# Expert routing over quads of tiles: a deeper software pipeline, and its row-wise passes on ScalarE

## The chip, the cores and the metric

The kernel runs on one core of one Trainium2 chip. The metric is the device time of the whole program in microseconds (us). Engine names in the profile: PE is TensorE, DVE is VectorE, ACT is ScalarE, POOL is GpSimd, SP is SyncE (here it only issues DMAs). Each engine runs its own instructions in the order in which they are written; between engines there are only semaphores.

## The reference

The model is a token encoder, an attention layer and a mixture-of-experts layer over 16 x 256 = 4096 tokens of width 128. The change touches only the routing of the last layer: a layer norm, 64 logits per token, a softmax, the 42 largest probabilities of 64, and a second softmax over those 42.

```python
h = h + _L0_ffn_ref(_layernorm(h, axis=-1), w1, b1, w2, b2, router_w, router_b)

def _L0_ffn_ref(x, w1, b1, w2, b2, router_w, router_b):     # E, H, K = (64, 256, 42)
    logits = x @ router_w + router_b
    probs = jax.nn.softmax(logits, axis=-1)
    top_w, top_idx = jax.lax.top_k(probs, K)
    top_w = jax.nn.softmax(top_w, axis=-1)
    ...
    comb = jnp.zeros((N, E), x.dtype).at[jnp.arange(N)[:, None], top_idx].set(top_w)
    h = jax.nn.gelu(jnp.einsum('td,edh->teh', xt, w1) + b1, approximate=False)
    y = jnp.einsum('teh,ehd->ted', h, w2) + b2
    out = jnp.einsum('ted,te->td', y, comb)
```

## The kernel before

The program is a row of blocks, one after the other: embedding, projections, attention, `route`, `experts`. Between two blocks all engines meet at a barrier. `h` holds the residual stream, 32 tiles of 128 tokens x 128, and `mv` each token's mean and variance.

`route` goes over 8 quads of 4 tiles (`QT = 4`, `GT = 512` tokens). For a quad q:

- DVE `norm` (L1501): four passes of 128x128 give the normed tiles `r_xn`.
- PE `turn_x` (L1571): four transposes into PSUM `r_ps_x`.
- ACT `copy_x` (L1459, L1460): PSUM to `x_s` and again to `x_hi` (the high part for the experts). POOL (L1482) makes `x_lo`.
- PE `logit` (L1579, L1580): for each tile one matmul with the router's weights and one with its bias (a contraction of one row). In the trace each of the 8 matmuls is two instructions.
- DVE `probabilities`: the negative row maximum (L1510), `d1` = logits less the maximum (L1512); ACT takes the exponent of it for the whole quad, 128x256 (L1470); DVE sums (L1515), takes the reciprocal (L1516), the negated probabilities `neg_p` (L1517) and `d2` (L1518); ACT takes the second exponent (L1473).
- DVE `choose`: with `neg_p` it finds the 22 experts to drop, 8 at a time, by MAX8 and MATCH_REPLACE8 (L1536, L1538). It then masks the second exponent (`top`, L1543), sums it (L1545), takes the reciprocal `r2` (L1546) and multiplies (`comb`, L1548).
- PE `turn_comb` (L1588): four transposes; ACT `copy_comb` (L1465) copies to `comb_t`, and SP writes it to the DRAM array `comb_rows` (L1438).

What runs beside what is set by the order in which each engine's steps are written. DVE's pass over quad q is max, `d1`, `norm(q + 1)`, sum to `d2`, `choose(q)`; PE's is `turn_x(q)`, `logit(q)`, `turn_comb(q - 1)`; ACT's is `copy_x(q)`, first exponent of q, `copy_comb(q - 1)`, second exponent of q. Two quads are written out, then a register loop runs over pairs of quads (`repeat`); on DVE the last two are written out again. `hold` is a wait followed by a no-op when the awaited value is in a register.

SP has in its queue, ahead of the rows: the loads of the router's weights and of the first experts' weights. After the rows of quads 0 to 3 it loads four 1 MB tiles `c_row` (L1642), broadcast from `comb_rows`, then writes the rows of quads 4 to 7. POOL splits two experts' weights (`split_weights`) after its last `x_lo`.

`experts` then makes three-part matmuls of 512 columns over 64 experts in two sweeps, and nothing of it is touched.

Of the kernel before, what the change touches and what calls it, by code (L numbers as in the profile page):

```python
# [7 lines left out]
F32 = mybir.dt.float32  # L8
# [3 lines left out]
ALU = mybir.AluOpType  # L12
# [1350 lines left out]
def route(nc, h, ident, ones_row, router_rev, router_b_rev, mv, rstd, x_hi, x_lo, comb_t, comb_rows, f, loader):  # L1363

    QT = GT // P
    QUADS = TILES // QT
    with ExitStack() as ctx:
# [9 lines left out]
        root = sb("r_root", [P, TILES])  # L1383
        xn = sb("r_xn", [P, 2, QT, DIM])
        x_s = sb("x_s", [P, 2, GT])
        neg_max = sb("r_neg_max", [P, QT])
        d1 = sb("d1", [P, QT, EXPERTS])
        e1 = sb("e1", [P, QT, EXPERTS])
        neg_s1 = sb("neg_s1", [P, QT])
        neg_r1 = sb("neg_r1", [P, QT])  # L1390
        neg_p = sb("neg_p", [P, QT, EXPERTS])
        d2 = sb("d2", [P, QT, EXPERTS])
        e2 = sb("e2", [P, QT, EXPERTS])
        left = sb("left", [P, QT, EXPERTS])
        low = sb("low", [P, QT, 8])
        top = sb("top", [P, QT, EXPERTS])
        s2 = sb("s2", [P, QT])
        r2 = sb("r2", [P, QT])
# [7 lines left out]
        rstd_ready = sem("r_rstd_ready")  # L1406
# [7 lines left out]
        d1_ready = sem("d1_ready")  # L1414
        exp_one = sem("exp_one")
        d2_ready = sem("d2_ready")
        exp_two = sem("exp_two")
        sum_step = sem("sum_step")
        top_step = sem("top_step")
        comb_ready = sem("comb_ready")  # L1420
# [4 lines left out]
        def cols(q):  # L1425
            return bass.ds(q * GT, GT)

        def spread(of_tile):
            return of_tile[:].unsqueeze(2).broadcast_to([P, QT, EXPERTS])
# [21 lines left out]
        @block.scalar  # L1451
        def _(act):
            act.wait_ge(var_eps, 1)
            act.activation(root[:], shifted[:], ACT.Sqrt).then_inc(rooted, 1)

            def copy_x(q, b):
                act.wait_ge(turned, q + 1)
                after(act, x_used, q - 1)
                act.activation(x_s[:, b], ps_x[:, b], ACT.Copy).then_inc(x_copied, 1)  # L1459
                act.activation(x_hi[:, cols(q)], ps_x[:, b], ACT.Copy).then_inc(hi_ready, 1)  # L1460

            def copy_comb(q, b):
                if in_range(q, QUADS):
                    hold(act, comb_turned, q + 1)
                    act.activation(comb_t[:, cols(q)], ps_c[0:EXPERTS, b], ACT.Copy).then_inc(comb_copied, 1)  # L1465
# [10 lines left out]
            copy_comb(QUADS - 1, 1)  # L1476

        @block.gpsimd
        def _(pool):
            def step(q, b):  # L1480
                pool.wait_ge(hi_ready, q + 1)
                pool.tensor_tensor(x_lo[:, cols(q)], x_s[:, b], x_hi[:, cols(q)].bitcast(F32), ALU.subtract  # L1482
                                   ).then_inc(x_used, 1)

            repeat(pool, step, QUADS)
            for r in range(SPLIT_EARLY):
                split_weights(pool, f, r, r, 32)

        @block.vector
        def _(dve):  # L1490
            dve.tensor_scalar(shifted[:], mv[:, :, 1], LN_EPS, None, ALU.add).then_inc(var_eps, 1)
            dve.wait_ge(rooted, 1)
            dve.reciprocal(rstd[:], root[:]).then_inc(rstd_ready, 1)
            dve.wait_ge(rstd_ready, 1)

            def norm(q, b):
                if in_range(q, QUADS):
                    after(dve, turned, q - 1)
                    for k in range(QT):
                        t = q * QT + k  # L1500
                        last = dve.tensor_scalar(xn[:, b, k, :], h[:, t, :], mv[:, t, 0:1], rstd[:, bass.ds(t, 1)],  # L1501
                                                 ALU.subtract, ALU.mult)
                    last.then_inc(normed, 1)

            def probabilities(q, b):

                of_quad = ps_l[:, b, 0:QT * EXPERTS].rearrange("p (k e) -> p k e", k=QT)
                link = chained(dve, sum_step, q * 3)
                dve.wait_ge(logits, q + 1)
                dve.tensor_reduce(neg_max[:], of_quad, AX.X, ALU.max, negate=True).then_inc(max_ready, 1)  # L1510
                hold(dve, max_ready, q + 1)
                dve.tensor_tensor(d1[:], of_quad, spread(neg_max), ALU.add).then_inc(d1_ready, 1)  # L1512
                norm(q + 1, 1 - b)
                dve.wait_ge(exp_one, q + 1)
                link(dve.tensor_reduce(neg_s1[:], e1[:], AX.X, ALU.add, negate=True))  # L1515
                link(dve.reciprocal(neg_r1[:], neg_s1[:]))  # L1516
                link(dve.tensor_tensor(neg_p[:], e1[:], spread(neg_r1), ALU.mult))  # L1517
                dve.tensor_tensor(d2[:], neg_p[:], spread(neg_r1), ALU.subtract).then_inc(d2_ready, 1)  # L1518

            def choose(q, b):  # L1520

                halves = (range(0, QT // 2), range(QT // 2, QT))
                before = q * STEPS
                rounds = [(taken, op) for taken in range(0, DROPPED, 8) for op in ("max", "marks", "take")
                          if op != "marks" or DROPPED - taken < 8]
                for n, (taken, op) in enumerate(rounds):
                    source = left if taken else neg_p
                    for half, tiles in enumerate(halves):
                        if n:
                            hold(dve, top_step, before + (2 * (n - 1) + half + 1))  # L1530
# [8 lines left out]
                        last.then_inc(top_step, 1)  # L1539
                link = chained(dve, top_step, before + 2 * len(rounds))  # L1540
                hold(dve, top_step, before + 2 * len(rounds))
                dve.wait_ge(exp_two, q + 1)
                link(dve.scalar_tensor_tensor(out=top[:], in0=left[:], scalar=MARK, in1=e2[:], op0=ALU.is_gt,  # L1543
                                              op1=ALU.mult))
                link(dve.tensor_reduce(s2[:], top[:], AX.X, ALU.add))  # L1545
                link(dve.reciprocal(r2[:], s2[:]))  # L1546
                after(dve, comb_turned, q - 1)
                dve.tensor_tensor(comb[:, b], top[:], spread(r2), ALU.mult).then_inc(comb_ready, 1)  # L1548

            def step(q, b):  # L1550
                if not isinstance(q, int) or q > 0:
                    hold(dve, comb_ready, q)
                probabilities(q, b)
                choose(q, b)

            ROUNDS = -(-DROPPED // 8)
            STEPS = 2 * (2 * ROUNDS + 1) + 3
            norm(0, 0)
            repeat(dve, step, QUADS - 2)
            for q in (QUADS - 2, QUADS - 1):  # L1560
                step(q, q % 2)

        @block.tensor
        def _(pe):
            pe.wait_ge(loads, 32)

            def turn_x(q, b):
                pe.wait_ge(normed, q + 1)
                after(pe, hi_ready, q - 1)
                for k in range(QT):  # L1570
                    last = pe.transpose(ps_x[:, b, k * P:(k + 1) * P], xn[:, b, k, :], ident[:])  # L1571
                last.then_inc(turned, 1)
# [347 lines left out]
```

## Time and profile before

| | us |
|---|---|
| runs, median of 3 | 2085.62 (2084.45 to 2085.73) |
| the profiled execution, its own time | 2084.88 |
| its span in the trace | 2083.0 |
| blocks before `route` | 0 to 571.2 |
| `route` | 571.2 to 662.5 |
| `experts` | 662.5 to 2083.0 |

Reading it: the profiled execution took 1.88 us more than the span of its trace, and its time lies 0.74 us under the median. The trace's rows show for each instruction its start and its duration; a row with x4 merges four instructions, and its duration is from the first start to the last end. In brackets stands the engine's idle time before the row and what ended it. The granted TensorE clock is given as a share of 2.4 GHz, so 0.50 is 1.2 GHz.

### The profile page before, as it was taken

What the parts mean: (1) busy time and instruction counts of PE and PEld (TensorE: products, weight loads), DVE (VectorE), ACT (ScalarE), POOL (GpSimd) and SP (SyncE); (2) the same over time, 40 slices, a digit from 0 to 9 for tenths busy, and PEclk for the clock granted to TensorE, in tenths of its full rate; (3) what the DMA queues carried; (4) which work ended last, traced back from release to release, by engine and by line L of the source; (5) the groups of instructions that cost most, each with busy time, mean ns of one, the idle gap of its engine ahead of it and who ended that gap; (6) DMA issues with size and microseconds to landing.
All of it is one profiled execution on the core that took longest, in us unless ns stands there. A gap on an engine that the chain in (4) does not pass through costs nothing.

```text
span 2083.0 us, 29167 instructions
## 1 busy us (share of the span) xinstructions
PE 1844.9 (89%) x8486; PEld 1461.0 (70%) x8486; DVE 1828.0 (88%) x2358; ACT 1454.8 (70%) x2558; POOL 682.5 (33%) x439
## 2 busy tenths in 40 slices
PE   5455658878766999999999999999999999999998
PEld 3333335555554888888888888878888888888887
DVE  8435558888677999999999999979999999999997
ACT  2145546666522888888888888878888888888886
POOL 4250015445312233333333333323333333333330
PEclk9967769899955999999999999999999999999999
DMA  7410000000012333333333333323333333333331
GB/s 207 136 41 0 1 1 1 0 0 0 1 34 96 126 121 108 124 126 126 113 113 126 126 124 109 119 101 126 117 112 124 126 126 111 116 126 126 123 108 56
DMA packets 105256, 191.46 MB, mean 92 GB/s; under 512 B 13558, under 2 KB 86246, under 8 KB 88550
## 3 DMA queue, kind: packets, MB, share of 16 engines
q1 hardware_dynamic: 103166, 186.77, 26.1%
q0 software_dynamic: 2048, 4.20, 0.7%
q8 instruction: 18, 0.29, 0.1%
q14 instruction: 24, 0.20, 0.0%
HBM read 179.40 MB, written 11.53 MB: 92 GB/s over the span
## 4 chain that ended last, share of the span: by engine, by line
PE 67%; DVE 0%; issue 0%; ACT 0%; DVEq 0%; ACTq 0%
PE f_ps_h L1837 11%; PE f_ps_h L1838 11%; PE f_ps_h L1839 11%; PE f_ps_y L1848 11%; PE f_ps_y L1849 11%; PE f_ps_y L1850 11%; PE f_ps_y L1863 0%; DVE s_lo L1793 0%; DVE scaled L1787 0%; PE f_ps_h L1874 0%; ACT act_out L1748 0%; DVE h L1811 0%; ACT y_t L1772 0%; DVEq L1669 0%; PE f_ps_h L1819 0%
## 5 line engine op out<-in xcount | busy, mean ns | idle before, releaser
L1748 ACT ACTIVATE act_out<-f_ps_h,b_t 128x512 f32<-128x512 f32 x1024 | 649.6, 686 | 257.4 <-PE f_ps_h L1839 257.4
L1787 DVE TENSOR_TENSOR scaled<-act_out,c_row 128x1024 f32<-128x1024 f32 x512 | 753.0, 1471 | 42.7 <-ACT act_out L1748 42.2
L1793 DVE TENSOR_TENSOR s_lo<-scaled,s_hi 128x1024 fp32r<-128x1024 f32 x512 | 672.7, 1314 | 0.1
L1756 ACT ACTIVATE s_hi<-scaled 128x1024 fp32r<-128x1024 f32 x512 | 541.9, 1058 | 2.3 <-DVE scaled L1787 1.5
L1651 POOL CAST w_hi<-w_raw 128x512 fp32r<-128x512 f32 x128 | 200.7, 1568 | 909.8 <-PE f_ps_y L1850 898.0
L1837 PE MATMUL f_ps_h<-x_hi,w_hi 128*128 x1024 | 399.8, 390 | 2.2 <-DVE h L1811 1.5
L1848 PE MATMUL f_ps_y<-s_hi,w_hi 128*128 128x512 f32 x1024 | 398.7, 389 | 3.0 <-DVE s_lo L1793 3.0
L1838 PE MATMUL f_ps_h<-x_lo,w_hi 128*128 x1024 | 399.4, 390 | 0.0
L1839 PE MATMUL f_ps_h<-x_hi,w_lo 128*128 x1024 | 399.2, 390 | 0.0
L1850 PE MATMUL f_ps_y<-s_hi,w_lo 128*128 128x512 f32 x1024 | 398.4, 389 | 0.0
L1849 PE MATMUL f_ps_y<-s_lo,w_hi 128*128 128x512 f32 x1024 | 398.4, 389 | 0.0
L1653 POOL TENSOR_TENSOR w_lo<-w_raw,w_hi 128x512 fp32r<-128x512 f32 x128 | 271.0, 2117 | 10.2
L1837 PEld LDWEIGHTS f_ps_h<-x_hi,w_hi 128*128 128x128 f32 x1024 | 192.7, 188 | 44.1 <-issue 4.1
L1848 PEld LDWEIGHTS f_ps_y<-s_hi,w_hi 128*128 128x128 f32 x1024 | 192.2, 188 | 44.5 <-DVE s_lo L1793 4.6
L1839 PEld LDWEIGHTS f_ps_h<-x_hi,w_lo 128*128 128x128 f32 x1024 | 192.8, 188 | 40.2
L1838 PEld LDWEIGHTS f_ps_h<-x_lo,w_hi 128*128 128x128 f32 x1024 | 192.8, 188 | 39.9
L1850 PEld LDWEIGHTS f_ps_y<-s_hi,w_lo 128*128 128x128 f32 x1024 | 192.2, 188 | 40.0
L1849 PEld LDWEIGHTS f_ps_y<-s_lo,w_hi 128*128 128x128 f32 x1024 | 192.2, 188 | 39.6
L1203 POOL TENSOR_TENSOR sm<-sm,rinv 128x1024 f32<-128x1024 f32 (+1 forms) x32 | 88.1, 2752 | 122.3 <-DVE rinv L1258 122.3
L1168 ACT ACTIVATE sm<-sm,neg_max 128x128 f32<-128x128 f32 (+1 forms) x256 | 112.7, 444 | 16.4 <-DVE neg_max L1252 16.3
L1189 POOL TENSOR_TENSOR qkn<-qk,rms 128x640 f32 (+1 forms) x32 | 40.3, 1260 | 158.4 <-SPq L1089 149.1
L1160 ACT ACTIVATE p_t<-ps_p 128x1024 f32<-128x1024 f32 x48 | 49.1, 1023 | 59.4 <-PE ps_p L1296 59.4
(219 smaller groups left out, 1652.7 us busy)
## 6 DMA issues: line engine op xcount, KB each, us to landing
c_row<-comb_rows SPq DMA_DIRECT2D x128, 1024.0 KB, 4.8
w_raw<-in_w SPq DMA_DIRECT2D x256, 128.0 KB, 4.3
by_slot<-b_zeros SPq DMA_DIRECT2D x1, 3072.0 KB, 13.4
b_gauss_s<-by_slot SPq DMA_DIRECT2D x12, 256.0 KB, 5.3
mixed_rows<-b_mixed SPq DMA_DIRECT2D x12, 256.0 KB, 2.3
out<-h SPq DMA_DIRECT2D x8, 256.0 KB, 4.7
cent<-in_centers SPq DMA_DIRECT2D x1, 1536.0 KB, 7.1
neg_prec<-in_logvar SPq DMA_DIRECT2D x1, 1536.0 KB, 10.9
```

The source lines that it names most:

```text
L1651: pool.tensor_copy(w_hi[:, r], w_raw[:, r]).then_inc(f["hi_copied"], 1)
L1653: pool.tensor_tensor(w_lo[:, r], w_raw[:, r], w_hi[:, r].bitcast(F32), ALU.subtract).then_inc(f["w_split"], 1)
L1748: last = act.activation(act_out[:, r % 2, c, :], ps_h[:, r % 2, c, :], ACT.Gelu, bias=b1_t[:, c, bass.ds(e, 1)])
L1756: act.activation(s_hi[:, r % RING], scaled[:, r % RING], ACT.Copy).then_inc(hi_ready, 1)
L1787: dve.tensor_tensor(scaled[:, r % RING], act_out[:, r % 2], c_row[:, k, g * GT:(g + 1) * GT].unsqueeze(1).broadcast_to([P, HC, GT]), ALU.m ...
L1793: dve.tensor_tensor(s_lo[:, r % RING], scaled[:, r % RING], s_hi[:, r % RING].bitcast(F32), ALU.subtract).then_inc(lo_ready, 1)
L1837: pe.matmul(to, w_hi[:, k, 0, at], x_hi[:, tokens(w, g)], start=True, stop=False)
L1838: pe.matmul(to, w_hi[:, k, 0, at], x_lo[:, tokens(w, g)], start=False, stop=False)
L1839: last = pe.matmul(to, w_lo[:, k, 0, at], x_hi[:, tokens(w, g)], start=False, stop=True)
L1848: pe.matmul(ps_y[:, g, :], w_hi[:, k, 1, at], s_hi[:, slot, c, :], start=False, stop=False)
L1849: pe.matmul(ps_y[:, g, :], w_hi[:, k, 1, at], s_lo[:, slot, c, :], start=False, stop=False)
L1850: last = pe.matmul(ps_y[:, g, :], w_lo[:, k, 1, at], s_hi[:, slot, c, :], start=False, stop=last_step and c == HC - 1)
```

## The change

Nothing is computed differently up to rounding. The register loops go: all 8 quads are written out on every engine. These steps move from DVE to ACT, and the 128x256 exponents are cut into one instruction for each tile, since ACT's scale and bias operands hold one number per row:

- `norm`: ACT.Identity with scale `rstd` and a new bias `r_shift` = -mean x rstd (one DVE pass of 128x32 at the start).
- `first_exps`: the exponent reads PSUM with the negative maximum as bias, and sums its row by `accum_out`; `d1` and DVE's sum (L1515) go. One small DVE pass of 128x4 turns s1 into -s1.
- `second_exps`: bias `neg_r1` takes the place of `d2`.
- `weigh`: ACT multiplies `top` by `r2` and gives `comb`.

A one-element exponent (`warm`) after the square root has the exponent's table loaded at once. The buffers between these steps are doubled. In line numbers of the changed kernel:

```diff
-            def step(q, b):
-                copy_x(q, b)
-                act.wait_ge(d1_ready, q + 1)
-                act.activation(e1[:], d1[:], ACT.Exp).then_inc(exp_one, 1)
-                copy_comb(q - 1, 1 - b)
-                act.wait_ge(d2_ready, q + 1)
-                act.activation(e2[:], d2[:], ACT.Exp, scale=-1.0).then_inc(exp_two, 1)
-            repeat(act, step, QUADS)
+            act.activation(warm[:], shifted[:, 0:1], ACT.Exp, scale=0.0)
+            def norm(q):
...
+                    act.wait_ge(ln_ready, 1)
+                    after(act, turned, q - 1)
+                    for k in range(QT):
+                        t = q * QT + k
+                        last = act.activation(xn[:, q % 2, k, :], h[:, t, :], ACT.Identity, scale=rstd[:, t:t + 1],
+                                              bias=shift[:, t:t + 1])
+                    last.then_inc(normed, 1)
+            def first_exps(q):
...
+                    act.wait_ge(max_ready, q + 1)
+                    for k in range(QT):
+                        last = act.activation(e1[:, b, k, :], ps_l[:, b, k * EXPERTS:(k + 1) * EXPERTS], ACT.Exp,
+                                              bias=neg_max[:, b, k:k + 1], accum_out=s1[:, b, k:k + 1])
+                    last.then_inc(exp_one, 1)
+            def second_exps(q):
...
+                    act.wait_ge(p_ready, q + 1)
+                    for k in range(QT):
+                        last = act.activation(e2[:, b, k, :], neg_p[:, b, k, :], ACT.Exp, scale=-1.0,
+                                              bias=neg_r1[:, b, k:k + 1])
+                    last.then_inc(exp_two, 1)
+            def weigh(q):
...
+                    act.wait_ge(r2_ready, q + 1)
+                    after(act, comb_turned, q - 1)
+                    for k in range(QT):
+                        last = act.activation(comb[:, b, k, :], top[:, b, k, :], ACT.Copy, scale=r2[:, b, k:k + 1])
+                    last.then_inc(comb_ready, 1)
+            norm(0)
+            copy_x(0)
+            norm(1)
+            first_exps(0)
+            copy_x(1)
+            second_exps(0)
+            norm(2)
+            for s in range(QUADS + 2):
+                first_exps(s + 1)
+                copy_x(s + 2)
+                weigh(s - 1)
+                norm(s + 3)
+                copy_comb(s - 2)
+                second_exps(s + 1)
...
+            maximum(0)
+            probabilities(0)
+            for q in range(QUADS):
+                maximum(q + 1)
+                after(dve, comb_ready, q - 1)
+                choose(q)
+                probabilities(q + 1)
...
+            turn_x(0)
+            logit(0)
+            turn_x(1)
+            logit(1)
+            for s in range(QUADS + 1):
+                turn_x(s + 2)
+                logit(s + 2)
+                turn_comb(s - 1)
```

How the instructions stand on ACT before, one quad inside the register loop (the names in brackets are the semaphores waited for):

```order
L1459 ACTIVATE x_s<-r_ps_x 128x512 [waits x_used,r_turned]
L1460 ISA
L1460 ACTIVATE x_hi<-r_ps_x 128x512
L1470 ACTIVATE e<-d 128x256 [waits d1_ready]
L1465 REGISTER_ALU [waits comb_turned]
L1465 ACTIVATE comb_t<-r_ps_c 64x512 [waits comb_turned]
L1473 ACTIVATE e<-d 128x256 [waits d2_ready]
```

And on ACT after the change, one pass in the middle (s = 2, so the rows are of quads 3, 4, 1, 5, 0 and 3):

```order
L1476 ACTIVATE e,s<-ps_l,r_neg_max 128x64 [waits r_max_ready]
L1476 ACTIVATE e,s<-ps_l,r_neg_max 128x64 x3
L1468 ACTIVATE x_s<-r_ps_x 128x512 [waits x_used,r_turned]
L1469 ACTIVATE x_hi<-r_ps_x 128x512
L1495 ACTIVATE comb<-top,r 128x64 [waits r2_ready]
L1495 ACTIVATE comb<-top,r 128x64 x3
L1459 ACTIVATE r_xn<-h,r_shift,rstd 128x128 [waits r_turned,r_ln_ready]
L1459 ACTIVATE r_xn<-h,r_shift,rstd 128x128 x3
L1501 ACTIVATE comb_t<-r_ps_c 64x512 [waits comb_turned]
L1485 ACTIVATE e<-neg_p,neg_r 128x64 [waits p_ready]
L1485 ACTIVATE e<-neg_p,neg_r 128x64 x3
```

ACT goes from 5 to 19 activations for a quad, and `x_s` of quad q + 2 now stands behind the first exponents of quad q + 1.

On DVE before, from the end of `choose(0)` to the start of `choose(1)`:

```order
L1543 SCALAR_TENSOR_TENSOR top<-left,e 128x256 [waits exp_two,top_step]
L1545 TENSOR_REDUCE s<-top 128x4 [waits top_step]
L1546 RECIPROCAL r<-s 128x4 [waits top_step]
L1548 TENSOR_TENSOR comb<-top,r 128x256 [waits top_step]
L1510 TENSOR_REDUCE r_neg_max<-ps_l 128x4 [waits logits,comb_ready]
L1512 TENSOR_TENSOR d<-ps_l,r_neg_max 128x256 [waits r_max_ready]
L1501 TENSOR_SCALAR r_xn<-h,mv,rstd 128x128 [waits r_turned]
L1501 TENSOR_SCALAR r_xn<-h,mv,rstd 128x128 x3
L1515 TENSOR_REDUCE neg_s<-e 128x4 [waits exp_one]
L1516 RECIPROCAL neg_r<-neg_s 128x4 [waits sum_step]
L1517 TENSOR_TENSOR neg_p<-e,neg_r 128x256 [waits sum_step]
L1518 TENSOR_TENSOR d<-neg_p,neg_r 128x256 [waits sum_step]
```

On DVE after the change, from the end of `choose(1)` to the start of `choose(2)`, the last row being the first MAX8:

```order
L1579 SCALAR_TENSOR_TENSOR top<-left,e 128x256 [waits exp_two,top_step]
L1581 TENSOR_REDUCE s<-top 128x4 [waits top_step]
L1582 RECIPROCAL r<-s 128x4 [waits top_step]
L1549 SCALAR_TENSOR_TENSOR neg_s<-s 128x4 [waits exp_one]
L1551 RECIPROCAL neg_r<-neg_s 128x4 [waits p_step]
L1552 TENSOR_TENSOR neg_p<-e,neg_r 128x256 [waits p_step]
L1540 TENSOR_REDUCE r_neg_max<-ps_l 128x4 [waits logits]
L1573 MAX low<-neg_p 128x8 [waits p_ready,comb_ready]
```

Eight passes have left DVE between two searches (four of them `norm`), one small one has come, and the maximum of quad q + 1, with its wait for the logits, now stands ahead of `choose(q)`.

## Rows read from the trace of the kernel before

**Rows 1.** Busy time, granted clock and DMA of two stretches: `route`, and `experts`.
```profile
core 0: us, PE busy (x) PEld busy (x) DVE busy (x) ACT busy (x) POOL busy (x), PEclk, DMA share, GB/s
571.20:662.50 91.30, 57.10 (x192) 41.93 (x192) 71.77 (x418) 21.68 (x43) 13.99 (x12) 0.51 0.20 70
662.50:2083.00 1420.50, 1408.97 (x6194) 1160.53 (x6194) 1366.64 (x1033) 1140.88 (x1546) 467.67 (x252) 1.00 0.33 116
```
**Rows 2.** The list of waits in `route`: total us, times, longest.
```profile
DVE r_neg_max L1510 <- PE ps_l L1580: 7.9, 3, 7.0
```
**Rows 3.** Timeline, start of `route`: start us, duration us, engine, instruction.
```profile
571.28 1.28 ACT L1454 ACT_TABLE_LOAD   x1 [5.67 <-PEq L1089]
...
572.58 0.23 ACT L1454 ACTIVATE r_root<-r_shifted 128x32 f32<-128x32 f32 x1
...
576.26 0.69 PE L1579 MATMUL ps_l<-rw,x_s 128*128 128x64 f32 x2 [0.69 <-ACT x_s L1459]
...
576.71 1.28 ACT L1470 ACT_TABLE_LOAD   x1
...
581.30 0.42 DVE L1510 TENSOR_REDUCE r_neg_max<-ps_l 128x4 f32<-128x256 f32 x1 [6.96 <-PE ps_l L1580]
```
**Rows 4.** Timeline of the last quad and the end of `route`.
```profile
651.08 0.43 DVE L1510 TENSOR_REDUCE r_neg_max<-ps_l 128x4 f32<-128x256 f32 x1
...
653.92 0.60 DVE L1536 MAX8 low<-neg_p 128x8 f32<-128x64 f32 x4
...
658.04 0.43 DVE L1543 SCALAR_TENSOR_TENSOR top<-left,e 128x256 f32<-128x256 f32 x1
...
659.17 0.43 DVE L1548 TENSOR_TENSOR comb<-top,r 128x256 f32<-128x256 f32 x1
...
659.74 1.03 PE L1588 MATMUL r_ps_c<-ident,comb 128*64 128x128 f32 x4 [7.51 <-DVE comb L1548]
660.81 0.59 ACT L1465 ACTIVATE comb_t<-r_ps_c 64x512 f32<-64x512 f32 x1 [6.36 <-PE r_ps_c L1588]
```
**Rows 5.** Timeline of PE inside the register loop, one quad.
```profile
625.28 0.69 PE L1579 MATMUL ps_l<-rw,x_s 128*128 128x64 f32 x2 [1.49 <-ACT x_s L1459]
...
629.60 0.69 PE L1580 MATMUL ps_l<-rb,ones_row 1*128 1x64 f32 x2
630.61 1.03 PE L1588 MATMUL r_ps_c<-ident,comb 128*64 128x128 f32 x4 [0.33 <-DVE comb L1548]
632.67 1.11 PE L1571 MATMUL r_ps_x<-ident,r_xn 128*128 128x128 f32 x4 [1.03 <-DVE r_xn L1501]
```
**Rows 6.** Groups of instructions in `route`: busy us, mean ns, idle before.
```profile
L1516 DVE RECIPROCAL neg_r<-neg_s 128x4 f32<-128x4 f32 x8 | 1.4, 178 | 0.6
L1517 DVE TENSOR_TENSOR neg_p<-e,neg_r 128x256 f32<-128x256 f32 x8 | 3.4, 425 | 0.6
L1459 ACT ACTIVATE x_s<-r_ps_x 128x512 f32<-128x512 f32 x8 | 4.7, 586 | 2.8 <-PE r_ps_x L1571 2.8
```
**Rows 7.** Timeline of ACT in attention: exponents with bias and row sum, 128x128.
```profile
509.29 0.39 ACT L1168 ACTIVATE sm<-sm,neg_max 128x128 f32<-128x128 f32 x1
509.59 0.19 ACT L1168 ACTIVATION_READ_ACCUMULATOR sm<-sm,neg_max 128x1 f32 x1
509.68 0.39 ACT L1168 ACTIVATE sm<-sm,neg_max 128x128 f32<-128x128 f32 x1
```
**Rows 8.** Timeline of ACT in the projections: a scaled copy of 64 columns.
```profile
151.22 0.31 ACT L881 ACTIVATE qk<-p_ps_rkv,p_kv_rms 128x64 f32<-128x64 f32 x1
151.42 0.23 ACT L882 ACTIVATE qk<-p_ps_rkv 128x64 f32<-128x64 f32 x1
```
**Rows 9.** Group, whole trace: ACT's layer norm of the projections.
```profile
L842 ACT ACTIVATE p_xn<-h,p_shift,p_rstd 128x128 f32<-128x128 f32 x32 | 13.7, 565 | 0.4 <-DVE p_shift L927 0.4
```
**Rows 10.** Timeline of DVE while POOL splits weights.
```profile
649.65 1.40 DVE L1548 TENSOR_TENSOR comb<-top,r 128x256 f32<-128x256 f32 x1
```
**Rows 11.** SP's issue of the four `c_row` loads, and the stretch in which they land.
```profile
624.99 2.00 SPq L1642 DMA_DIRECT2D c_row<-comb_rows  x4
...
625.00:637.00 12.00, 8.79 (x30) 6.64 (x30) 10.71 (x71) 3.09 (x7) 2.28 (x2) 0.50 0.91 360
```

More of the change, by code:

```diff
@@ L1505, in probabilities @@
[L1505 to L1518, printed above, removed]
@@ L1538, in choose @@
                                 last = dve.match_replace(left[:, k, :], low[:, k, :], source[:, k, :], MARK)
-                        last.then_inc(top_step, 1)
-                link = chained(dve, top_step, before + 2 * len(rounds))
-                hold(dve, top_step, before + 2 * len(rounds))
+                        mark(last)
+                settle()
                 dve.wait_ge(exp_two, q + 1)
-                link(dve.scalar_tensor_tensor(out=top[:], in0=left[:], scalar=MARK, in1=e2[:], op0=ALU.is_gt,
+                link(dve.scalar_tensor_tensor(out=top[:, b], in0=left[:], scalar=MARK, in1=e2[:, b], op0=ALU.is_gt,
                                               op1=ALU.mult))
[L1545 to L1561, printed above, removed]
+                link(dve.tensor_reduce(s2[:], top[:, b], AX.X, ALU.add))
+                dve.reciprocal(r2[:, b], s2[:]).then_inc(r2_ready, 1)
+            maximum(0)
+            probabilities(0)
+            for q in range(QUADS):
+                maximum(q + 1)
+                after(dve, comb_ready, q - 1)
+                choose(q)
+                probabilities(q + 1)
         @block.tensor
@@ L1565, in _ @@
             pe.wait_ge(loads, 32)
[L1567 to L1572, printed above, removed]
-            def logit(q, b):
-                pe.wait_ge(x_copied, q + 1)
-                after(pe, d1_ready, q - 1)
-                for k in range(QT):
-                    of_tile = ps_l[:, b, k * EXPERTS:(k + 1) * EXPERTS]
-                    pe.matmul(of_tile, x_s[:, b, k * P:(k + 1) * P], rw[:], start=True, stop=False)
-                    last = pe.matmul(of_tile, ones_row[:], rb[:], start=False, stop=True)
-                last.then_inc(logits, 1)
@@ L1583, in turn_comb, with turn_x, logit @@
-            def turn_comb(q, b):
+            def turn_x(q):
+                if in_range(q, QUADS):
+                    pe.wait_ge(normed, q + 1)
+                    after(pe, hi_ready, q - 1)
+                    for k in range(QT):
+                        last = pe.transpose(ps_x[:, q % 2, k * P:(k + 1) * P], xn[:, q % 2, k, :], ident[:])
+                    last.then_inc(turned, 1)
+            def logit(q):
+                if in_range(q, QUADS):
+                    b = q % 2
+                    pe.wait_ge(x_copied, q + 1)
+                    after(pe, exp_one, q - 1)
+                    for k in range(QT):
+                        of_tile = ps_l[:, b, k * EXPERTS:(k + 1) * EXPERTS]
+                        pe.matmul(of_tile, x_s[:, b, k * P:(k + 1) * P], rw[:], start=True, stop=False)
+                        last = pe.matmul(of_tile, ones_row[:], rb[:], start=False, stop=True)
+                    last.then_inc(logits, 1)
```

111 lines of the change are left out of this document (63 added, 48 removed).

## The prediction

> **What bounds the kernel now.** I read the windows by stage first [rows 1]. `route` takes 91.3 us of 2083, PE's clock is granted at 0.51 there (1.2 GHz), and DVE is the busiest engine with 71.8 us; in `experts` PE is busy for 1409 of 1420.5 us at 1.00. Nothing in `experts` is edited, so the change is worth what it takes off `route`. The list of waits says who drives it [rows 2]: DVE waited 7.9 us in all for logits, 7.0 of them before the first quad. From then on DVE hardly stops, so DVE's own pass is the pace. The timeline gives that pace: the first of eight row maxima starts at 581.30 [rows 3], the last at 651.08 [rows 4]: 69.78 us for 7 quads, 9.97 each. So `route` before is a start (571.28 to 581.30), 69.78 us of pace, and a tail from the last maximum to the end of the last ACT copy (651.08 to 661.40, 10.32 us) [rows 4]. I cost each of the three.
>
> **The pace after the change.** Four loops could set it. I take each from rows and keep the longest; M(q) is the start of quad q's maximum.
>
> *DVE's pass.* Maximum 0.43 + 0.04 of gap. From the first MAX8 to the masked exponent 4.12 (653.92 to 658.04), from there to the end of `r2` 1.10 (to just before 659.17) [rows 4]. Then the small pass of 128x4, which no row here shows and which I take as the reciprocal of the same shape, 0.18, the reciprocal 0.18, and `neg_p` 0.43 [rows 6], with gaps 0.9. Sum 6.6 us.
>
> *PE's pass.* The eight steps of the logits are issued 0.617 apart (625.28 to 629.60 is seven of them), so 4.93; four `comb` transposes last 1.03 alone and four `x` transposes 1.11 [rows 5]. In a queue the first four give way earlier: one transpose alone is some 0.42 of the 1.03, so four follow each other in 0.82. PE's queue is still `turn_x`, `logit`, `turn_comb`, and between `turn_x` and `logit` of one quad stands ACT's copy `x_s`, 0.59 [rows 6]. PE has no other quad's work to put there. Sum 4.93 + 0.82 + 1.11 + 0.59 + 0.1 for two hand-overs = 7.55 us.
>
> *The loop through ACT.* `x_s` of quad q + 2 is queued behind the first exponents of q + 1, and these behind M(q + 1). An exponent with row sum starts 0.39 after the one before at 128 columns (509.29 to 509.68) [rows 7]; I take 0.33 at 64, four in 1.33. Bounds for the four are 1.33 and 4 x (0.39 + 0.19) = 2.3 if nothing overlaps. Maximum 0.43 + 1.33 + `x_s` 0.59 + logits and hand-over 5.04 (576.26 to 581.30) [rows 3] + 0.1 = 7.5 us. It is level with PE's pass.
>
> *The loop over two quads.* ACT's second exponents of q + 1 wait for DVE's pass, and ahead of `x_s` of q + 3 stand they and the first exponents of q + 2. A scaled copy of 64 columns lets the next start after 0.20 and lasts 0.31 [rows 8], so four in 0.93. DVE's pass 6.6 + 0.93 + 1.42 + 0.59 + 5.04 = 14.6 for two quads, 7.3 each. It is closed, but 0.25 a quad short of deciding.
>
> ACT's own work, overlapped, is 1.33 + 1.1 (two copies) + 0.85 + 1.7 (`norm`: 13.7 us for 32 [rows 9]) + 0.55 + 0.85 = 6.4 us. It has a reserve of 1.1 us per quad.
>
> So PE and its round trip to ACT take over from DVE: 7 x 7.55 = 52.9 us in place of 69.8, **-16.9 us**. What DVE gave away above 0.9 us per quad is not earned. Removing the register loops is in these numbers, since I used the rows of the written-out last quad.
>
> **Two rules weighed.** Does PE stay at 1.2 GHz? PE runs 6.0 us of logits and transposes with one gap of 0.33 (625.28 to 631.64) [rows 5], eight times over, and the clock's mean over the block stays 0.51 [rows 1]. After the change the same instructions run with fewer gaps, so I keep 1.2 GHz. The Trainium skill (TensorE: Matmul & The Clock Gate, "What's actually happening") says that sustained matmul activity releases the throttle. By it the clock would rise, now that PE's gaps shrink, and the sum would be that of the first rival below. The Trainium skill (ScalarE: Activation LUTs, "Rules for kernel authors") advises VectorE, not ScalarE, for multiplications and additions. For the work itself the trace agrees: 256 columns are 0.43 us on DVE [rows 6] and 0.93 in four pieces on ACT [rows 8]. It costs here only where ACT is on the path, which is the tail.
>
> **The start, later.** The root ends at 572.81 [rows 3]. The exponent's table load of 1.28, hidden under the logits before (576.71) [rows 3], now stands ahead of `norm(0)`: 574.1, plus the one-element exponent, 0.2 by the root beside it. `norm(0)` on ACT takes 13.7 / 32 x 4 = 1.7: 576.0. Transposes 1.11, `x_s` 0.59, logits 5.04 and hand-overs: M(0) = 582.9. That is **+1.6 us**. DVE then waits before `choose(0)`, since the maximum of quad 1 stands ahead of it. M(1) is still one loop through ACT later (7.5), so this wait moves work into the tail and does not lengthen the pace.
>
> **The tail, longer.** `choose(6)`, which before lay ahead of the last maximum, now lies behind it. From M(7): maximum 0.47, `choose(6)` 5.27, probabilities 0.85, `choose(7)` 5.22, `weigh` on ACT 0.93 (0.43 on DVE before), transposes 1.03, copy 0.59, hand-overs 0.15: 14.5 us in place of 10.3, **+4.2 us**. Here the first exponents and `comb`'s copies have no cover at all; all else on ACT is covered by DVE's search.
>
> **Moved and hidden.** POOL's weight split slows DVE passes with two tensors: `comb` took 1.40 in place of 0.43 beside it [rows 10]. It now falls near the sixth quad, where DVE has 0.9 us of reserve; I take 0, with 0.7 late if it misses. SP's `c_row` loads wait for `comb` of quad 3. They were issued at 624.99 and took about 12 us [rows 11]. `comb_t` of quad 3 now leaves near 632 and is written by 635, so they land near 647, before `experts` starts near 650. What is queued behind them on SP is only the writing of rows of the second sweep. The waits `exp_one` and `comb_ready` on PE and DVE are met 3 us early in this schedule. If the burst slows something, it costs at most what it lasts beyond 650: nothing to 3 us.
>
> **Sum.** +1.6 - 16.9 + 4.2 = -11.1 us. Against the profiled execution's own 2084.88 that is 2073.8; against the median of the runs, 0.74 higher, 2074.5. I say **2074.2**. With a pace of 7.45 to 7.95 (hand-overs smaller, or 0.4 more each quad) this case runs from 2073 to 2077.5.
>
> **Rivals.**
>
> 1. *PE's clock rises.* Then PE's pass shrinks (logits between half of 5.04 and 5.04) and DVE's 6.6 is the pace from M(1): 7.5 + 6 x 6.6 = 47.1, -22.7. Sum -16.9: **2068**. For it: PE's gaps shrink to one of 0.65 us in a pass. Against: eight stretches of 6 us without a rise. Chance 0.14.
> 2. *The passes run longer than their parts*, 8.5 in place of 7.55: hand-overs on a three-engine loop, ACT starting its pieces later than the 0.33, written-out code that must be fetched while `c_row` fills the DMA engines (share 0.91 [rows 11]). 59.5 of pace, -10.3; sum -4.5: **2080**. For it: with three loops within 0.25 us of each other, a delay in any is felt. Against: written-out quads showed no gaps. Chance 0.14.
> 3. *Slower: ACT becomes the bound.* If its short instructions do not overlap, ACT pays whole durations for a quad: first exponents 2.3, two copies 1.2, `weigh` 1.24, `norm` 4 x 0.565 = 2.26 [rows 9], `copy_comb` 0.59, second exponents 1.24, with hand-overs 9.1. Pace 63.7 (-6.1), start +2.1, tail +5.4: sum +1.4, **2086**. It decides for slower from an ACT pass of 8.9 us on, and beyond 0.2% from 9.5. Against it: rows 7 and 8 show overlap on this engine, in the same forms. Chance 0.06.
> 4. *The pipeline does not engage.* If each quad's exponents, search and logits still came one after the other, the loop of 14.6 would be one quad's: far slower. ACT's order has two quads in it, so I give it 0.01, with nothing else behind it.
>
> **How the numbers follow.** The forecast has 0.65, the rivals 0.14, 0.14, 0.06 and 0.01. The predicted time is the forecast's. The range 2067 to 2079 takes in the forecast, most of rival 1 and the nearer part of rival 2, and leaves out some 2 in 10. A change of this kernel's time under 0.2% (4.2 us) cannot be told from none. Rival 3 has 0.05 within that bound and 0.01 beyond it, and of rival 2 some 0.02 comes within it: faster 0.91, same 0.07, slower 0.02.
>
> **What would show it.** In the trace after, maxima should start 7.5 to 7.6 apart, the first near 582.9 and the last near 636; the list of waits in `route` should have DVE waiting for the logits in every quad (0.9 each, and 4 to 5 before the second), and PE for `x_s` 0.65 each. The windows should still show 0.5 of clock. `experts` should be as long as before, to 1 us. I am wrong if the spacing is 6.6 (clock), or if ACT shows no idle time before its first exponents.

## The result, and the profile after

The changed kernel takes 2073.45 us, median of 5 runs (2071.74 to 2074.41), against 2085.62 before (5 runs, 2084.45 to 2085.87): a ratio of 0.9943, with a 95% interval of 0.9928 to 0.9957. That is 12.2 us, where 2074.2 was forecast in a range of 2067 to 2079. The profiled execution took 2071.74, its span is 2070.0, 13.0 less than before. One run of a later kernel ("bias once" in the table below) was slow, 10046 us; its ratio leaves that run out, its median of four does not.

The windows by stage of the changed kernel, to be held against [rows 1]: busy time of each engine, granted clock, DMA.

```profile
core 0: us, PE busy (x) PEld busy (x) DVE busy (x) ACT busy (x) POOL busy (x), PEclk, DMA share, GB/s
571.20:649.40 78.20, 55.71 (x192) 42.55 (x192) 50.01 (x363) 53.67 (x188) 13.87 (x12) 0.51 0.23 81
649.40:2070.00 1420.60, 1408.23 (x6194) 1160.50 (x6194) 1366.47 (x1033) 1140.18 (x1546) 467.53 (x252) 1.00 0.33 116
```

By these edges `route` is 13.1 us shorter. The edges are rough: 649.40 lies 0.94 us ahead of the first matmul of `experts` (650.34), and 662.50 in the kernel before lies 0.08 ahead of it. Cut at instructions, as in the table below, it is 12.0 us shorter. DVE is busy 50.0 us in it, 21.8 less, and ACT 53.7, 32.0 more. PE's busy time is nearly what it was (55.7 for 57.1), at the same granted clock (1.2 GHz): PE is now the busiest engine of the stage, with ACT close to it. The list of waits says the same. Columns are total us, times, longest.

```profile
DVE r_neg_max L1540 <- PE ps_l L1612: 20.5, 8, 9.4
...
ACT e L1476 <- DVE r_neg_max L1540: 8.8, 7, 3.5
...
PE ps_l L1611 <- ACT x_s L1468: 7.3, 8, 1.3
```

Before, DVE waited for logits 7.9 us, nearly all ahead of the first quad [rows 2]; now it waits in all eight quads. The engine from which work was taken has turned from the one that sets the pace into one that waits.

The timeline shows the new pace. Of the eight row maxima of DVE, six:

```profile
582.54 0.42 DVE L1540 TENSOR_REDUCE r_neg_max<-ps_l 128x4 f32<-128x256 f32 x1 [9.39 <-PE ps_l L1612]
...
589.87 0.42 DVE L1540 TENSOR_REDUCE r_neg_max<-ps_l 128x4 f32<-128x256 f32 x1 [4.71 <-PE ps_l L1612]
...
597.20 0.42 DVE L1540 TENSOR_REDUCE r_neg_max<-ps_l 128x4 f32<-128x256 f32 x1 [1.05 <-PE ps_l L1612]
...
612.06 0.42 DVE L1540 TENSOR_REDUCE r_neg_max<-ps_l 128x4 f32<-128x256 f32 x1 [1.26 <-PE ps_l L1612]
...
619.59 0.42 DVE L1540 TENSOR_REDUCE r_neg_max<-ps_l 128x4 f32<-128x256 f32 x1 [1.26 <-PE ps_l L1612]
...
634.66 0.42 DVE L1540 TENSOR_REDUCE r_neg_max<-ps_l 128x4 f32<-128x256 f32 x1 [0.48 <-PE ps_l L1612]
```

The first three steps are 7.33 us, the last four 7.53; together 52.12 where [rows 3] and [rows 4] gave 69.78. One pass of PE, with ACT's part of it (the columns are start, duration, engine, instruction, idle before):

```profile
612.80 1.06 PE L1601 MATMUL r_ps_x<-ident,r_xn 128*128 128x128 f32 x4
614.55 0.69 PE L1611 MATMUL ps_l<-rw,x_s 128*128 128x64 f32 x2 [0.69 <-ACT x_s L1468]
...
618.87 0.69 PE L1612 MATMUL ps_l<-rb,ones_row 1*128 1x64 f32 x2
619.48 1.06 PE L1620 MATMUL r_ps_c<-ident,comb 128*64 128x128 f32 x4
620.34 1.06 PE L1601 MATMUL r_ps_x<-ident,r_xn 128*128 128x128 f32 x4
622.09 0.69 PE L1611 MATMUL ps_l<-rw,x_s 128*128 128x64 f32 x2 [0.69 <-ACT x_s L1468]
```

```profile
612.52 0.31 ACT L1476 ACTIVATE e<-ps_l,r_neg_max 128x64 f32<-128x64 f32 x1 [0.62 <-DVE r_neg_max L1540]
612.73 0.19 ACT L1476 ACTIVATION_READ_ACCUMULATOR e<-ps_l,r_neg_max 128x1 f32 x1
612.82 0.30 ACT L1476 ACTIVATE e<-ps_l,r_neg_max 128x64 f32<-128x64 f32 x1
...
613.90 0.60 ACT L1468 ACTIVATE x_s<-r_ps_x 128x512 f32<-128x512 f32 x1
```

From logits to logits it is 614.55 to 622.09, 7.54 us: 4.93 of logits, 0.86 of `comb` transposes, 1.06 of `x` transposes, and one gap of 0.69 us in which PE has only `x_s` to wait for. ACT starts that copy at 613.90, just after the transposes end (613.86) and just after its own four exponents: the two paths to `x_s` are nearly level. The end of the block, to be held against [rows 4]:

```profile
646.29 1.06 ACT L1495 ACTIVATE comb<-top,r 128x64 f32<-128x64 f32 x4 [2.83 <-DVE r L1582]
...
648.57 0.59 ACT L1501 ACTIVATE comb_t<-r_ps_c 64x512 f32<-64x512 f32 x1 [0.74 <-PE r_ps_c L1620]
```

The tail, from the last maximum to the end of this copy, is 14.50 us, where it was 10.32.

### The profile page after: what moved, and what is told of

The parts are those of the page before. It is cut to its first block, busy times and chain, and to the rows that moved or that the text cites. A ratio compares the mean times of both kernels' runs of the same rounds, so it can differ in the third digit from the quotient of the medians.

```text
span 2070.0 us, 29016 instructions
## 1 busy us (share of the span) xinstructions
PE 1840.7 (89%) x8486; PEld 1459.9 (71%) x8486; DVE 1806.2 (87%) x2303; ACT 1486.1 (72%) x2703; POOL 682.3 (33%) x439
## 4 chain that ended last, share of the span: by engine, by line
PE 68%; DVE 0%; issue 0%; ACT 0%; DVEq 0%; ACTq 0%
PE f_ps_h L1870 11%; PE f_ps_h L1871 11%; PE f_ps_h L1872 11%; PE f_ps_y L1881 11%; PE f_ps_y L1883 11%; PE f_ps_y L1882 11%; PE f_ps_y L1896 0%; DVE s_lo L1826 0%; DVE scaled L1820 0%; PE f_ps_h L1907 0%; ACT act_out L1781 0%; DVE h L1844 0%; ACT y_t L1805 0%; DVEq L1702 0%; PE f_ps_h L1852 0%
```

## The experiments

Each kernel's `route` was cut in its trace nearly as in the prediction: start (from the square root on ACT, which is 1.3 us after its table load, where the prediction began, to the first maximum), pace (first to last of the eight maxima), tail (to the end of the last `comb_t` copy). "Total" is their sum, "experts" what follows from the first matmul of that block. All in us; each figure is a difference of two starts or ends in the timeline. The ratio is to the kernel before on the same chip, whose median was 2086.0 for the four kernels "loops" to "bias once" and 2086.12 for the three after them.

| kernel | start | pace | tail | total | experts | median | ratio (95%) |
|---|---|---|---|---|---|---|---|
| before | 8.72 | 69.78 | 10.32 | 88.82 | 1420.42 | 2085.62 | |
| changed | 10.23 | 52.12 | 14.50 | 76.85 | 1419.66 | 2073.45 | 0.9943 (0.9928 to 0.9957) |
| loops written out only | 8.73 | 67.23 | 10.31 | 86.27 | 1420.06 | 2084.08 | 0.9993 (0.9984 to 1.0003) |
| depth, loops written out | 8.72 | 60.52 | 15.32 | 84.56 | 1421.45 | 2082.21 | 0.998 (0.997 to 0.9989) |
| moves, loops written out | 10.25 | 71.89 | 10.85 | 92.99 | 1420.08 | 2090.82 | 1.0027 (1.0017 to 1.0038) |
| bias once | 8.36 | 43.63 | 14.48 | 66.47 | 1419.92 | 2063.74 | 0.9892 (0.9873 to 0.9912) |
| turns earlier | 10.66 | 45.50 | 14.49 | 70.65 | 1420.96 | 2068.39 | 0.9912 (0.9895 to 0.9929) |
| 12 constant matmuls at the start | 8.34 | 52.14 | 14.50 | 74.98 | 1420.51 | 2071.31, one run | |
| and one ahead of each quad's logits | 8.35 | 52.12 | 14.50 | 74.97 | 1420.51 | 2073.63, one run | |
| start and tail taken back | 8.86 | 52.16 | 13.86 | 74.88 | 1420.61 | 2095.75 | 0.9933 (0.9916 to 0.9949) |
| all together | 7.54 | 42.54 | 13.84 | 63.92 | 1420.80 | 2085.02 | 0.988 (0.9863 to 0.9896) |
| changed, again | 10.24 | 52.13 | 14.50 | 76.87 | 1419.64 | 2095.75 | 0.9932 (0.9919 to 0.9946) |
| all together, again | 7.54 | 42.52 | 13.85 | 63.91 | 1420.87 | 2084.97 | 0.9884 (0.9869 to 0.99) |

The last four rows come from two other chips, two rows from each. Both ran what lies ahead of `route` some 20 us slower, in the kernel before too (2110.63 on the first, 2109.19 on the second), so there the ratio and the parts are to be read, not the median. The parts of `route` repeat to 0.02 us between the two traces of a kernel, and so separate these kernels better than their times do.

**What paid: the depth, the moves, or the loops?** The first kernel does one thing alone: it is the kernel before with its loops written out. The two after it do one thing more each, the depth or the moves, with the loops written out as well, so they are to be held against the first and not against the kernel before.

```diff
-            repeat(act, step, QUADS)
+            for q in range(QUADS):
+                step(q, q % 2)
```

(and so on POOL, DVE and PE.)

> The kernel before, with nothing changed but that the register loops of route are written out over the 8 quads. My theory: written-out quads of before were 9.4 to 9.5 us apart, those in the loop 10.0 to 10.4, so the maxima come 9.45 to 9.6 apart, start and tail stay, and the time falls by 3 to 3.5 us, to 2082.3. The rival, that the loops were most of what was saved, asks for 8 us or more off: 2077 or less.

The maxima are 9.46 apart in six steps, as expected, and 10.44 in the last, where POOL splits weights. `route` is 2.6 us shorter. The time is 1.9 us under its kernel before, with an interval that takes in no change; the parts show the gain, the times alone do not. About a fifth of what the change took off `route` is in the loops; the rival falls. DVE waits 0.51 us for the logits in each of the first six steps of this kernel, so its own pass (8.95) is not all of the step.

Depth without moves, ScalarE's new steps back on DVE in the new order (an edit of the changed kernel, cut here to DVE's main loop):

```diff
             for q in range(QUADS):
                 maximum(q + 1)
-                after(dve, comb_ready, q - 1)
+                norm(q + 3)
                 choose(q)
                 probabilities(q + 1)
```

> The changed kernel's depth (norm three quads ahead, logits two, everything written out), with all row-wise passes back on VectorE as before. My theory: VectorE's pass is 6.3 plus d1 0.46, norm 1.1, the larger sum 0.3, d2 0.46 and comb 0.46, so 9.1 us, and the tail keeps choose(6) behind the last maximum: pace 63.4, start as before, tail +5; the time is 2084 to 2085. The rival, that the depth is what paid: 2075 or less.

Steps of 8.87 us, and DVE waits for logits only ahead of the first two maxima. The pace is 60.5 where 63.4 was expected, and the tail grows by 5.0 as expected. Against the loops written out alone the pace falls by 6.7 and the tail grows by 5.0: `route` is 1.7 us shorter. The rival, 2075 or less, falls with 2082.2.

Moves without depth (also an edit of the changed kernel, cut to ACT's main loop; DVE and PE go back to the order of before too):

```diff
+            for q in range(QUADS):
+                first_exps(q)
+                norm(q + 1)
+                copy_comb(q - 1)
+                second_exps(q)
+                copy_x(q + 1)
+                weigh(q)
```

> The changed kernel's passes on ScalarE, everything written out, but in the order of before: each engine finishes quad q before the next, logits one quad ahead only. My theory: norm(q + 1) then stands behind the first exponents of q, and turn, copy and logits behind it, so maxima are 10.2 us apart whatever VectorE has given away: pace +1.6, start +1.5, tail as before; the time is 2087 to 2089. The rival, that taking work off VectorE is what paid: VectorE's pass with its wait for the exponents is 7.9 us, and the time about 2074.

Steps of 10.29 us and a slower kernel: 2090.8, where 2087 to 2089 was expected and the rival asked for 2074. The pace grew by 2.1 for an expected 1.6, and the tail by 0.5 for none. One quad of its timeline shows the chain:

```profile
614.24 0.42 DVE L1536 TENSOR_REDUCE r_neg_max<-ps_l 128x4 f32<-128x256 f32 x1 [2.32 <-PE ps_l L1606]
...
615.88 1.64 ACT L1459 ACTIVATE r_xn<-h,r_shift,rstd 128x128 f32<-128x128 f32 x4
...
617.57 1.12 PE L1595 MATMUL r_ps_x<-ident,r_xn 128*128 128x128 f32 x4 [2.38 <-ACT r_xn L1459]
...
618.85 0.59 ACT L1468 ACTIVATE x_s<-r_ps_x 128x512 f32<-128x512 f32 x1
...
619.49 0.69 PE L1605 MATMUL ps_l<-rw,x_s 128*128 128x64 f32 x2 [0.80 <-ACT x_s L1468]
...
624.53 0.42 DVE L1536 TENSOR_REDUCE r_neg_max<-ps_l 128x4 f32<-128x256 f32 x1 [2.32 <-PE ps_l L1606]
```

Maximum and exponents of one quad, then norm, transposes, copy and logits of the next, and its maximum: one behind the other, with DVE idle 2.3 us in each. The next quad's norm needs nothing of this quad's exponents; it stands behind them only in ACT's order. Held against the loops written out alone (86.27 for `route`), the depth takes 1.7 us, the moves add 6.7, and the two together take 9.4; the loops themselves gave the other 2.6 of the 12.0. The moves pay only once the order lets DVE run ahead, and the depth pays little while DVE has the work. No kernel separates the doubled buffers and the early table load from these; both halves have them.

**What sets the pace now?** The router's bias is added by one matmul of 256 columns in place of four of 64:

```diff
...
+                    pe.matmul(ps_l[:, b, 0:QT * EXPERTS], ones_row[:], rb[:], start=True, stop=False)
                     for k in range(QT):
                         of_tile = ps_l[:, b, k * EXPERTS:(k + 1) * EXPERTS]
-                        pe.matmul(of_tile, x_s[:, b, k * P:(k + 1) * P], rw[:], start=True, stop=False)
-                        last = pe.matmul(of_tile, ones_row[:], rb[:], start=False, stop=True)
+                        last = pe.matmul(of_tile, x_s[:, b, k * P:(k + 1) * P], rw[:], start=False, stop=(k == QT - 1))
```

> The changed kernel, with the router's bias added by one matmul of 256 columns for a quad in place of four of 64. My theory, that PE's pass and its round trip to ScalarE set the pace (7.45 us): the logits shorten by some 1.4 us a quad, the pace falls until VectorE's pass of 6.3 us holds it, 6.3 to 6.4, and the time falls by 7 to 8 us more, to 2066. The rival, that VectorE or ScalarE set the pace and their waits are only hand-overs: no change, 2073.5.

```profile
603.84 1.21 PE L1611 MATMUL ps_l<-rb,ones_row 1*128 1x256 f32 x2 [1.43 <-ACT x_s L1470]
604.99 1.97 PE L1614 MATMUL ps_l<-rw,x_s 128*128 128x64 f32 x8
606.75 1.06 PE L1622 MATMUL r_ps_c<-ident,comb 128*64 128x128 f32 x4
```

The logits take 3.1 us (603.84 to 606.96) and not 5.0. That is more than the bias alone: it now costs 1.15 in place of 2.47, and the four matmuls with the weights, which no longer alternate with it, are 0.44 apart (604.99 to 606.75 for four) in place of 0.62. The list of waits names DVE's only waits for the logits: two, 10.3 us in all, 7.5 ahead of the first maximum and 2.8 ahead of the second.

```profile
DVE r_neg_max L1542 <- PE ps_l L1614: 10.3, 2, 7.5
```

The spacing is 6.25 us from the third step to the sixth, DVE's pass, and the total falls by 10.4 us: 8.5 in the pace, 1.9 in the start, which my sum for this kernel had left out. DVE's passes were not touched, so the rival falls. The logits stand in PE's pass and in the loop through ACT alike, so this kernel does not tell the two apart. In its last step, 7.0 us, POOL's weight split costs 0.75, now that DVE has no slack.

The other way to the same end leaves the logits and fills the gap (again an edit of the changed kernel, cut to the main loops): transposes run three quads ahead, and ACT copies x before it takes exponents.

```diff
             for s in range(QUADS + 2):
-                first_exps(s + 1)
                 copy_x(s + 2)
+                first_exps(s + 1)
                 weigh(s - 1)
-                norm(s + 3)
+                norm(s + 4)
...
             for s in range(QUADS + 1):
-                turn_x(s + 2)
+                turn_x(s + 3)
                 logit(s + 2)
```

> The changed kernel with another order: norm four quads ahead, TensorE's transposes three ahead, and ScalarE copies x before it takes the first exponents, so that x_s is ready when TensorE comes to the logits. My theory: TensorE's gap of 0.7 us and the loop through ScalarE's exponents both go; TensorE's bare pass of 6.8 to 6.9 us is the pace, 48 us for seven in place of 52.1, and the time falls by 4 us from 2073.5 to 2069.5. The rival, that VectorE's or ScalarE's passes set the pace: no change.

```profile
610.32 1.06 PE L1602 MATMUL r_ps_x<-ident,r_xn 128*128 128x128 f32 x4
611.17 0.53 PE L1612 MATMUL ps_l<-rw,x_s 128*128 128x64 f32 x2
...
615.95 1.06 PE L1621 MATMUL r_ps_c<-ident,comb 128*64 128x128 f32 x4
```

The logits follow 0.85 behind the start of the transposes, without a gap, and the spacing is 6.48 in the fourth to sixth step (5.7, 6.2 and 6.8 before, 7.4 in the last, where POOL splits weights). I had 6.8 to 6.9. I had charged the `x` transposes their 1.1 us as if alone, while in a queue the next work starts after 0.85; and the logits, which start before the transposes end, take 4.78 to the next transposes (611.17 to 615.95) and not 4.93. The start is 0.4 us longer, since the transposes of quad 1 now stand ahead of the first logits.

**Would a faster clock have paid?** TensorE got 12 constant matmuls of 512 columns where it had waited for the first norm; the second kernel has these and one more ahead of each quad's logits.

```diff
+            def idle(n):
+                for _ in range(n):
+                    pe.matmul(ps_w[:], idle_w[:, 0:P], idle_w[:], start=True, stop=True)
+            idle(12)
...
+                    idle(1)
                     pe.wait_ge(x_copied, q + 1)
```

> The changed kernel with 12 matmuls of 512 columns on a constant tile (bf16, result unused) on TensorE at the start of route, where it waited 6.3 us for the first norm. My theory: the clock stays at 2.4 GHz through the gap, so the first logits run faster; then, with logits and transposes alone, the clock falls back to 1.2 GHz, since eight stretches of them never raised it, and route is shorter by 1 to 3 us. If the clock holds, TensorE's pass falls under VectorE's 6.3 us, and route takes 70 us in place of 78. The rival, that these matmuls do nothing for the clock: route as long as before them, 78 us.

> As the kernel with 12 constant matmuls at the start of route, and one more of 512 columns in front of each quad's logits, where TensorE waits 0.7 us for x_s. My theory has no firm forecast: if it holds the clock at 2.4 GHz, the pace falls to VectorE's 6.3 us and route takes about 70 us; if not, the matmul fits in the gap at 0.43 us and route stays at 76 to 78 us.

Of the first kernel, PE's timeline and the windows of 4 us:

```profile
572.11 4.16 PE L1602 MATMUL ps_w<-idle_w 128*128 128x512 bf16 x12 [2.15 <-POOL idle_w L1523]
...
579.61 0.43 PE L1624 MATMUL ps_l<-rb,ones_row 1*128 1x64 f32 x2
579.97 0.55 PE L1623 MATMUL ps_l<-rw,x_s 128*128 128x64 f32 x2
580.45 0.69 PE L1624 MATMUL ps_l<-rb,ones_row 1*128 1x64 f32 x2
```

```profile
576.00:580.00 4.00, 3.31 (x18) 2.46 (x17) 0.00 (x0) 2.72 (x7) 1.27 (x1) 0.91 0.87 245
580.00:584.00 4.00, 2.72 (x11) 2.05 (x10) 1.19 (x4) 2.37 (x11) 0.02 (x1) 0.52 0.05 15
584.00:588.00 4.00, 4.00 (x14) 3.21 (x14) 0.00 (x0) 2.43 (x8) 1.24 (x1) 0.50 0.00 0
```

The clock came back to 2.4 GHz and the first logits ran 0.36 us apart in place of 0.62. Two microseconds into them it fell, with PE at work on logits (its last gap, 0.69 us, had ended at 577.79), and it did not rise again in `route`. One matmul in each gap cost nothing and raised nothing: the granted clock of the second kernel is 0.50 in every window from 584 to 656. What was gained is 1.9 us in the start. So the pace stayed at 52.1 in both; that at 2.4 GHz it would fall to DVE's is argued, not shown. The kernel with its turns earlier bears on this too: from 604.70 to 629.00 PE was busy for 23.83 of 24.30 us with logits and transposes, and the granted clock was 0.50 throughout. Closing the gaps did not raise it.

**Start and tail.** `norm` of quad 0 and the last multiplication by `r2` go back to DVE.

```diff
...
+            for k in range(QT):
+                last = dve.tensor_scalar(xn[:, 0, k, :], h[:, k, :], mv[:, k, 0:1], rstd[:, k:k + 1],
+                                         ALU.subtract, ALU.mult)
+            last.then_inc(first_normed, 1)
...
+                    dve.tensor_tensor(comb[:, b], top[:, b], spread(r2[:, b]), ALU.mult).then_inc(comb_last, 1)
```

> The changed kernel with two moves taken back at the ends only: norm of the first quad on VectorE (while ScalarE loads the exponent's table), and the multiplication by r2 of the last quad on VectorE. My theory, by which start and tail are paid in full and the pace is TensorE's: the first maximum comes 1.3 us earlier, the tail is 0.5 us shorter, the spacing stays 7.45: 2071.7 where the changed kernel has 2073.5. The rival, that such moves are hidden everywhere: no change.

Start 1.37 less, tail 0.64 less, pace as it was: both ends are paid in full, the middle is not. The times do not show it. This kernel and the changed one were measured on different chips, so only their ratios can be compared, 0.9933 and 0.9932, and each interval is wider than the 0.1% in question (the runs of each spread over 5 to 6 us). The 2 us rest on the parts alone.

**All of it.** The edits above but for the constant matmuls, and DVE's first search ahead of the maximum of quad 1:

```diff
+            choose(0)
+            maximum(1)
+            maximum(2)
+            probabilities(1)
+            for q in range(1, QUADS):
+                if q > 1:
+                    maximum(q + 1)
```

> All together: one bias matmul for a quad, transposes three quads ahead, ScalarE's copies ahead of its exponents, norm of the first quad and the last multiplication on VectorE, and the first search (choose(0)) ahead of the maximum of quad 1. My theory: with TensorE's pass near 5 us VectorE's 6.25 us is the pace, as with the bias alone (2063.7), so the new order adds nothing there; the start gives 1.3, the tail 0.5, and the early first search 2.3 us: 2059.6, 26 us under the kernel before. The rival, that the pace is still TensorE's or ScalarE's somewhere: spacing under 6.2 or over 6.5 us.

> The changed kernel itself once more, beside the kernel with all edits together, because the chip of the last two kernels ran the program's first 130 us some 22 us slower, the kernel before too. Expected: 12 us under the kernel before, as measured first.

> The kernel with all edits together once more, on the same chip as the changed kernel. Expected: 13 us under the changed kernel, from its route block, which took 63.9 us from the square root to the last copy where the changed kernel's took 76.9; the rival, that part of this was that chip, gives less than 10.

`route` takes 63.9 us both times, 12.95 less than in the changed kernel and 24.9 less than before; 1.2 us go back in `experts`, where the clock rises later, and 10.8 us remain between the medians on the same chip. The ratio to before is 0.9884. DVE's steps are 6.18 us in the middle. The changed kernel itself came out 13.4 us under its kernel before, for 12 expected. The 10.8 lie between the 13 I expected and the rival's 10; the parts hold the 13 in `route`.

Against the bias alone `route` is 2.55 us better, and 0.9 of that goes back in `experts`; the ratios (0.9884 and 0.9892) do not separate the two. The ends gave 1.5 for the 1.8 expected: 0.8 in the start for 1.3, since the transposes of quad 1 stand ahead of the first logits here too, and 0.6 in the tail for 0.5. The pace gave only 1.1 (43.63 to 42.54) of the 2.3 that I gave the early search. Two waits stand beside that: DVE was idle 1.0 us for the exponents of quad 1 (before 611.37), and the last step took 7.72, 1.54 over the spacing where the bias alone paid 0.75, since POOL's split now fell beside two large passes of DVE (1.22 us for `top` and 1.16 for `neg_p`, 0.43 and 0.42 elsewhere).

## Why the prediction was right, point by point

- *DVE hands the pace to PE and its round trip to ACT.* Right, and shown twice: shortening the logits brought the step to DVE's 6.25, and closing PE's gap brought it to 6.48, with DVE's work unchanged. Which of the two nearly level loops decides a step is read from the spacing in the trace; no kernel shortens one of them alone.
- *PE's pass 7.55.* Measured 7.53 to 7.54, in the last four steps. *The loop through ACT 7.5.* Measured 7.33, in the first three, before `comb` transposes join PE's queue: the exponents follow each other in 0.29, not the 0.33 I took from [rows 7]. *DVE's pass 6.6.* Measured 6.28 (maximum 604.52, `neg_p` done 610.80) and 6.18 where it is the pace; the small pass takes 0.13 and the reciprocals give way early. So the pace came to 52.12 for my 52.9: -17.7 in place of -16.9. I took one loop for all seven steps, PE's; that the one through ACT set the first three is 0.66 of the 0.7 us.
- *Start +1.6.* Measured +1.51 (10.23 less 8.72). *Tail +4.2.* Measured +4.18. Inside it two terms missed and made up for each other: `weigh` took 1.06 for my 0.93, and DVE's part ahead of it 11.63 (634.66 to 646.29) for my 11.81.
- *POOL's split hidden.* Right. Three passes of DVE were slowed around the end of quad 5's search: `top` took 0.64 us (0.42 elsewhere), the pass of 128x4 0.56 (0.13) and `neg_p` of quad 6 0.57 (0.42). DVE's wait for the next logits shrank from 1.26 to 0.48, and the step stayed 7.54. With DVE as the pace it cost 0.75 with the bias alone, near the 0.7 named, but 1.54 in the kernel with all edits.
- *`c_row` in time.* Issued at 633.74; its transfers filled 634 to 646. `experts` began at 650.3, and no wait for it appears.
- *Clock stays at 1.2 GHz.* Right for `route`, from the first transposes to its end. By the first of the two rules weighed the clock should have risen as PE's gaps shrank; it did not, here or with the gaps closed (0.50 over 24 us of busy PE), and the measurement decides. The clock is the one thing that I left out of the sum elsewhere: in `experts` it rose sooner. Before and after:

```profile
663.67 0.79 PE L1837 MATMUL f_ps_h<-x_hi,w_hi 128*128 x1 [0.64 <-DVE b_t L1777]
...
668.52 0.45 PE L1839 MATMUL f_ps_h<-x_hi,w_lo 128*128 x1
```

```profile
651.43 0.79 PE L1870 MATMUL f_ps_h<-x_hi,w_hi 128*128 x1 [0.65 <-DVE b_t L1810]
...
654.58 0.51 PE L1871 MATMUL f_ps_h<-x_lo,w_hi 128*128 x1
654.93 0.40 PE L1872 MATMUL f_ps_h<-x_hi,w_lo 128*128 x1
```

  The duration falls 3.2 us after the first three-part matmul; before, it fell at 668.52, 4.9 us after 663.67. `experts` is 0.76 us shorter (1419.66 for 1420.42), and 0.71 of that has been gained by the end of the first twelve three-part matmuls (5.61 us from the block's first matmul for 6.32). Why the clock rose sooner is open; I did not forecast it, and in the kernel with all edits it rose later than before.
- *The sum.* `route` from the square root on: -11.97 for my -11.1; `experts` -0.76; the blocks ahead -0.27, which nothing in the change accounts for: the span's -13.0. PE's loop was off by 0.02 us, the one through ACT by 0.2 and DVE's by 0.3, all the same way. The profiled execution, the fastest of the five, lies 2.5 under my 2074.2 and the median 0.75: some of that closeness is chance, since the runs spread over 2.7 us.
- *Rivals.* The clock did not rise. The passes were shorter than their parts, not longer. ACT's instructions overlap as in [rows 7] and [rows 8], and it was idle 0.62 us ahead of its first exponents. The pipeline engaged. The second rule weighed, that additions and multiplications belong on VectorE, held while the order was the old one (the moves alone made `route` 6.7 us longer) and at both ends; in the middle of the deeper pipeline it did not.

## What to carry to other kernels

When work leaves the engine that sets the pace, the gain ends where the next loop begins: write down each loop through the engines (own pass, round trip, loop over two items) before counting what was moved. Here DVE gave up 2.7 us of busy time per quad (21.8 over eight) and its pass fell by 3.7 (9.97 to 6.28, with the loops' gaps and waits in it), but the step fell only by 2.5. The deeper order alone bought 1.7 us and the moves alone lost 6.7, where both together bought 9.4. An experiment that is to price one half of a change must be held against a kernel that shares the rest of it. At both ends of a pipeline there is no cover, so the moved work counts in full there, and a step may be left on the old engine for its first and last item.

## What the runs showed of the hardware that was not expected

- The clock fell from 2.4 to 1.2 GHz while PE was busy with fp32 logits of 64 columns, 4 us after the constant matmuls. Matmuls of 512 columns set singly into the stream did not bring it back (0.50 throughout), and neither did 24 us in which PE was 98% busy with such logits and transposes.
- In a queue four PE transposes of 128x128 at 1.2 GHz cost 0.85 us where the row of four alone shows 1.03 to 1.12; work priced by such a row is priced too high by a fifth to a third.
- Where they alternate, an fp32 bias of one row costs as much as a full matmul (0.62 us for 64 columns at 1.2 GHz). 256 columns of bias at once cost 1.15 where four of 64 cost 2.5, and the full matmuls, left to follow each other, cost 0.44 each and not 0.62.
